# A three-stage TensorE kernel on one core: projections in couples on halves of the rows, and the last tile's first row block in three parts

## What is computed

```python
Kf  = einsum('bjd,ed->bje', F, K_w)
S   = einsum('bid,bjd->bij', F, Kf)
out = einsum('bij,ijd->bid', S, W) + einsum('bid,ed->bie', F, Q_w)
```

## Time and profile before

| | |
|---|---|
| median of 3 runs | 607.16 us (607.0 to 607.43) |
| profiled execution, its own time | 606.42 us |
| its span, first to last instruction | 604.6 us |
| granted TensorE clock, mean | 0.998 of 2.4 GHz |
| busy: TensorE, VectorE, ScalarE | 596.4, 399.2, 401.5 us |
| moved by DMA | 138.12 MB, mean 228 GB/s |

### The profile page before, as it was taken

One profiled execution on the slowest core, in us unless ns is written; L12 is line 12 of the kernel. 1 busy time (PEld: TensorE's weight loads), 2 busy tenths in 40 slices (PEclk: granted clock), 3 DMA queues, 4 the chain that ended last, 5 costly groups with the idle time before them and its releaser, 6 DMA issues.

```text
span 604.6 us, 17904 instructions
## 1 busy us (share of the span) xinstructions
PE 596.4 (99%) x7690; PEld 526.3 (87%) x7690; DVE 399.2 (66%) x412; ACT 401.5 (66%) x696; POOL 0.2 (0%) x4
## 2 busy tenths in 40 slices
PE   9999999999999999999999999999999999999995
PEld 7888989889898898988989898898988989889895
DVE  6556768567685675947749475685756768567486
ACT  7888393874938659295692947939387493865920
POOL 0000000000000000000000000000000000000000
PEclk9999999999999999999999999999999999999999
DMA  8644847457575575755657566484754857557177
GB/s 338 262 141 160 330 165 282 183 185 305 191 281 172 210 266 208 279 196 210 242 192 287 203 238 249 143 319 174 277 209 173 318 179 284 173 209 273 70 281 279
DMA packets 29452, 138.12 MB, mean 228 GB/s; under 512 B 3264, under 2 KB 3776, under 8 KB 21312
## 3 DMA queue, kind: packets, MB, share of 16 engines
q1 hardware_dynamic: 20736, 75.83, 31.8%
q10 hardware_dynamic: 8640, 61.15, 28.4%
HBM read 69.86 MB, written 67.11 MB: 227 GB/s over the span
## 4 chain that ended last, share of the span: by engine, by line
PE 98%; DVE 1%; issue 1%; DVEq 0%
PE ps L509 20%; PE ps L447 20%; PE ps L449 19%; PE ps L448 19%; PE ps L541 18%; DVE o_sb L372 1%; PE ps L576 1%; DVEq L49 0%; DVE o_sb L382 0%; PE ps L467 0%; PE ps L465 0%; PE ps L469 0%; DVE f_hi L388 0%; DVEq L115 0%
## 5 line engine op out<-in xcount | busy, mean ns | idle before, releaser
L337 DVE TENSOR_TENSOR f_lo<-f_ring,f_hi 128x1024 fp32r<-128x1024 f32 x124 | 151.8, 1224 | 168.2 <-ACT f_hi L217 166.6
L231 ACT ACTIVATE q_out<-ps 128x512 f32<-128x512 f32 x256 | 156.9, 613 | 6.6 <-PE ps L449 0.2
L222 ACT ACTIVATE kf<-ps 128x512 f32<-128x512 f32 x256 | 155.8, 609 | 3.5
L372 DVE TENSOR_TENSOR o_sb<-ps,q_out 128x1024 f32<-128x1024 f32 x127 | 145.1, 1215 | 19.4 <-PE ps L541 19.3
L240 ACT ACTIVATE s_t<-ps 128x512 f32<-128x512 f32 x32 | 19.1, 598 | 175.8 <-PE ps L509 175.8
L509 PE MATMUL ps<-f_ring,kf 128*64 128x64 f32 x4096 | 123.5, 222 | 0.3 <-issue 0.3
L509 PEld LDWEIGHTS ps<-f_ring,kf 128*64 128x64 f32 x4096 | 121.1, 138 | 2.6 <-issue 0.8
L541 PEld LDWEIGHTS ps<-s_t,w_sb 64*128 64x128 f32 x2048 | 115.6, 188 | 5.6 <-issue 5.6
L541 PE MATMUL ps<-s_t,w_sb 64*128 64x128 f32 x2048 | 118.6, 274 | 0.0
L447 PE MATMUL ps<-f_hi,k_hi 128*128 128x512 f32 x255 | 101.0, 396 | 0.0
L447 PE MATMUL ps<-f_hi,q_hi 128*128 128x512 f32 x256 | 100.0, 391 | 0.0
(11 more groups left out here) (39 smaller groups left out, 160.3 us busy)
## 6 DMA issues: line engine op xcount, KB each, us to landing
out<-o_sb SPq DMA_DIRECT2D x127, 512.0 KB, 3.5
f_ring<-f_t ACTq DMA_DIRECT2D x58, 1024.0 KB, 4.8
f_ring<-f_t SPq DMA_DIRECT2D x4, 1024.0 KB, 10.6
f_ring<-f SPq DMA_DIRECT2D x8, 256.0 KB, 5.3
w_sb<-w SPq DMA_DIRECT2D x1, 2048.0 KB, 17.8
out<-o_sb SPq DMA_DIRECT2D x2, 256.0 KB, 2.6
o_sb<-first SPq DMA_DIRECT2D x1, 192.0 KB, 2.9
o_sb<-first ACTq DMA_DIRECT2D x1, 192.0 KB, 3.4
```

The source lines that it names most:

```text
L222: nc.scalar.activation(kf[:, c // 2, c % 2 * CK:(c % 2 + 1) * CK, :, :].rearrange("d k h i -> d (k h i)"), ps[:, 2 * c % 8, :], COPY).then ...
L231: nc.scalar.activation(q_out[:, t % 2, :, :].rearrange("d i (h b) -> d i h b", h=2)[:, :, :, at:at + CK], q_bank(t * CHUNKS + c).rearrange ...
L337: nc.vector.tensor_tensor(f_lo[:, v % SPLIT, :], f_unit(v), f_hi[:, v % SPLIT, :].bitcast(F32), ALU.subtract).then_inc(flo_done, 1)
L372: nc.vector.tensor_tensor(o_sb[:, n % OBUF, :, :, :].rearrange("d x s b -> d s x b"), ps[:, bank:bank + 2, :].rearrange("d s (x b) -> d s ...
```

## The change

The projection of the tiles 1 to 15 is issued in couples. A couple is two matmuls of 64 rows each, one on the lower, one on the upper half of TensorE's rows, into two different banks. A chunk's two products (a: Q, b: K) are made in two halves of three couples: first a on the lower rows beside b on the upper rows, then b on the lower beside a on the upper. Between the two halves of chunk n - 1 stand the first halves of chunk n: the order is first(0), first(1), second(0), first(2), second(1), and so on, and at the end first(15), second(14), second(15). Each second half waits on TensorE for half_done. In the last tile, whose last two Q products still run later in the old form, the last step couples K of chunk 14 with K of chunk 15. Tile 0 keeps the old form.

FILL changes to 74, 220 and 284, and its waits lie between the chunks 3 to 15. The splits wait for k_done beside q_done. In the last tile ScalarE copies only the last Q product; the one before is copied by VectorE. The first row block of the last tile goes in three parts, row 0, row 1, and rows 2 and 3, to the banks 0, 2 and 6 (and the next odd ones), with three sums and three stores; the banks and waits of the blocks behind it change with that.

```diff
-FILL = {1: 0, 2: 56}
-FILL.update((t, 108) for t in range(3, TILES - 1))
-FILL[TILES - 1] = 132
+EARLY = 3
+FILL = {1: 74, 2: 220}
+FILL.update((t, 220) for t in range(3, TILES - 1))
+FILL[TILES - 1] = 284
...
-            return [0, 6, 4, 0, 2, 6, 4, 0][k] if t == TILES - 1 else 2 * k % 8
+            return [0, 4, 0, 2, 6, 4, 0, 2][k] if t == TILES - 1 else 2 * k % 8
+        block_0 = [(0, 1, 0), (1, 1, 2), (2, 2, 6)]
...
             def split_f(v):
                 act.wait_ge(q_done, 2 * (v - SPLIT) + 2)
+                act.wait_ge(k_done, 2 * (v - SPLIT) + 2)
...
-                act.wait_ge(k_done, t * CHUNKS + c + 1)
+                act.wait_ge(k_done, n + 1 if n < TILES * CHUNKS - LATE else TILES * CHUNKS)
...
-            for c in range(CHUNKS - LATE, CHUNKS):
-                copy_q(t, c)
+            copy_q(t, CHUNKS - 1)
...
+            c = CHUNKS - 2
+            at = c * CK
+            dve.wait_ge(q_done, TILES * CHUNKS - 1)
+            nc.vector.tensor_copy(
+                q_out[:, t % 2, :, :].rearrange("d i (h b) -> d i h b", h=2)[:, :, :, at:at + CK],
+                q_bank(t * CHUNKS + c).rearrange("d (k h i) -> d i h k", k=CK, h=2)).then_inc(q_copied_dve, 1)
+
             n = t * UNITS
-            dve.wait_ge(o_half, 1)
-            dve.wait_ge(q_copied, TILES * CHUNKS)
+            dve.wait_ge(q_copied, TILES * CHUNKS - 1)
+            dve.wait_ge(q_copied_dve, 1)
             dve.wait_ge(o_stored[n % OBUF], n // OBUF * 16)
-            half_sum(0).then_inc(out_half, 1)
+            for part in range(2):
+                dve.wait_ge(o_part, part + 1)
+                part_sum(part).then_inc(out_part, 1)
             dve.wait_ge(o_done, n + 1)
-            half_sum(1).then_inc(out_done, 1)
+            part_sum(2).then_inc(out_done, 1)
...
+            def products(step):
+                if step < TILES * CHUNKS - LATE:
+                    return (q_of(step), q_done), (k_of(step), k_done)
+                return (k_of(step), k_done), (k_of(step + 1), k_done)
...
+            def passes(dst, w_hi, w_lo, c, rows, first):
+                hi = f_hi[rows, c // 2 % SPLIT, piece_cols(c)]
+                lo = f_lo[rows, c // 2 % SPLIT, piece_cols(c)]
+                yield nc.tensor.matmul(dst, w_hi[rows, :], hi, start=first, stop=False)
+                yield nc.tensor.matmul(dst, w_hi[rows, :], lo, start=False, stop=False)
+                yield nc.tensor.matmul(dst, w_lo[rows, :], hi, start=False, stop=not first)
+
+            def first_halves(step):
+                (a, _), (b, _) = products(step)
+                for ins_a, ins_b in zip(passes(*a, lower, True), passes(*b, upper, True)):
+                    pass
+                ins_a.then_inc(half_done, 1)
+                ins_b.then_inc(half_done, 1)
+
+            def second_halves(step):
+                pe.wait_ge(half_done, 2 * (step - CHUNKS + 1))
+                (a, a_sem), (b, b_sem) = products(step)
+                for ins_b, ins_a in zip(passes(*b, lower, False), passes(*a, upper, False)):
+                    pass
+                ins_b.then_inc(b_sem, 1)
+                ins_a.then_inc(a_sem, 1)
...
+                    if c >= 4 and n < TILES * CHUNKS - LATE:
                         pe.wait_ge(q_copied, n - 3)
-                    if t < TILES - 1 or c < CHUNKS - LATE:
-                        q_product(n)
-                    if t >= 1:
-                        for x in range(FILL[t] * c // CHUNKS, FILL[t] * (c + 1) // CHUNKS):
-                            pe.wait_ge(zeros_done, 1)
+                    first_halves(n)
+
+                    if c >= 1:
+                        second_halves(n - 1)
+
+                    a, b = max(c - EARLY, 0), CHUNKS - EARLY
+                    for x in range(FILL[t] * a // b, FILL[t] * max(c + 1 - EARLY, 0) // b):
+                        pe.wait_ge(zeros_done, 1)
+                if t >= 1:
+                    second_halves(min((t + 1) * CHUNKS - 1, TILES * CHUNKS - LATE))
...
-                    at, col = (bank + 2 * (x // 2), x % 2 * P) if split else (bank, x * P)
+                    at, col = (block_0[min(x, 2)][2], max(x - 2, 0) * P) if split else (bank, x * P)
...
-                    if t == TILES - 1 and k >= 3:
-                        pe.wait_ge(out_half if k == 3 else out_done, 1 if k == 3 else t * UNITS + k - 3)
+                    if t == TILES - 1 and k in (2, 3):
+                        pe.wait_ge(out_part, k - 1)
...
-                    elif k == 2:
-                        pe.wait_ge(q_copied, TILES * CHUNKS)
+                    elif k == 1:
+                        pe.wait_ge(q_copied, TILES * CHUNKS - 1)
+                        pe.wait_ge(q_copied_dve, 1)
```

More of the change, by code:

```diff
@@ L97, in build @@
         fhi_done, flo_done = sem("fhi_done"), sem("flo_done")
+        half_done = sem("half_done")
+        q_copied_dve = sem("q_copied_dve")
         k_done, kf_copied = sem("k_done"), sem("kf_copied")
@@ L191, in _ @@
             slot = t * UNITS % OBUF
[L192 to L196, removed]
+            for part, (x, rows, _) in enumerate(block_0):
+                if part < 2:
+                    sp.wait_ge(out_part, part + 1)
+                else:
+                    sp.wait_ge(out_done, t * UNITS + 1)
+                sp.dma_start(out[t, 0, :, 2 * x * P:2 * (x + rows) * P],
+                             o_sb[:, slot, x:x + rows, :, :].rearrange("d x s b -> d (x s b)")).then_inc(o_stored[slot], 16)
             for k in range(1, UNITS):
@@ L199, in _ @@
             for n in range(OBUF):
-                uses = len(range(n, TILES * UNITS, OBUF)) + (1 if n == slot else 0)
+                uses = len(range(n, TILES * UNITS, OBUF)) + (2 if n == slot else 0)
                 sp.wait_ge(o_stored[n], 16 * uses)
@@ L208, in split_first @@
                 wait(act, q_done, 2 * (c // 2 - SPLIT) + 2)
+                wait(act, k_done, 2 * (c // 2 - SPLIT) + 2)
                 nc.scalar.activation(f_hi[:, c // 2 % SPLIT, piece_cols(c)], f_cols(c), COPY).then_inc(fhi_first, 1)
@@ L225, in copy_q @@
             def copy_q(t, c):
-                act.wait_ge(q_done, t * CHUNKS + c + 1)
+                n = t * CHUNKS + c
+                act.wait_ge(q_done, n + 1 if n < TILES * CHUNKS - LATE else TILES * CHUNKS)
                 if c == 0:
@@ L328, in both_first @@
                 wait(dve, q_done, 2 * (c // 2 - SPLIT) + 2)
+                wait(dve, k_done, 2 * (c // 2 - SPLIT) + 2)
                 if c == 4:
@@ L376, in sum_out, with part_sum @@
                     ALU.add).then_inc(out_done, 1)
-            def half_sum(half):
+            def part_sum(part):
                 t = TILES - 1
-                m = half * (IR // 2)
+                x, rows, bank = block_0[part]
                 return nc.vector.tensor_tensor(
-                    o_sb[:, t * UNITS % OBUF, m:m + IR // 2, :, :].rearrange("d x s b -> d s x b"),
-                    ps[:, 2 * half:2 * half + 2, 0:BANK // 2].rearrange("d s (x b) -> d s x b", x=IR // 2),
-                    q_out[:, t % 2, :, :].rearrange("d (s m) b -> d s m b", s=2)[:, :, m:m + IR // 2, :],
+                    o_sb[:, t * UNITS % OBUF, x:x + rows, :, :].rearrange("d x s b -> d s x b"),
+                    ps[:, bank:bank + 2, 0:rows * P].rearrange("d s (x b) -> d s x b", x=rows),
+                    q_out[:, t % 2, :, :].rearrange("d (s m) b -> d s m b", s=2)[:, :, x:x + rows, :],
                     ALU.add)
@@ L542, in row_block @@
                                                start=True, stop=True)
-                    if split and x == IR // 2 - 1:
-                        ins.then_inc(o_half, 1)
+                    if split and x < 2:
+                        ins.then_inc(o_part, 1)
                 ins.then_inc(o_done, 1)
```

22 lines of the change are left out of this document (17 added, 5 removed).

## The result

The change made the kernel slower, by 0.3%: 609.36 us median (606.97 to 610.68, 6 runs) against 607.58 for the kernel before (607.0 to 608.16, 6 runs), ratio 1.003, 95% interval 1.0018 to 1.0042. The forecast was 594.3 us, its range 590.0 to 606.3. The profiled execution took 606.97 us with a span of 605.2; it is the fastest of the six, so the trace shows 2.4 us less than the median run holds.

The account below looks back on a forecast made before the run. TensorE, busy 99% of the span, was taken to bound the kernel. Savings of 12.0 and 2.8 us less costs of 1.8 and 0.1 made 12.9 us, so 594.3 us from the median 607.16; range 590.0 to 606.3.

Parts of the forecast that it names:

- The couples (the main term): Projection on TensorE: coupled half-row matmuls step in 218.3 ns in place of 226.7, saving 12.0 us.
- no gain in the step: Projection: extra 13.4 ns may be the fp32r weight swap, so couples save nothing; 605.4 us, chance 0.17.
- The slower rival, halves one after the other: Projection: the two halves don't run side by side, a couple takes 431.7 ns; about 900 us, chance 0.03.
- The change of form: Between projection, row blocks and scores: 0.19 us of switching lost today goes, 15 times, saving 2.8 us.
- The late fifth sum: End of the row blocks: scores wait for VectorE's delayed fifth sum, 0.12 us, 14 times; 1.8 us given back.
- Instructions and code: TensorE's sequencer: more instructions and waits, about 78 code fetches; cost set at nothing, bounds -0.5 and +4 us.
- late code: Rival: code fetches stall TensorE 0.27 us at two borders in each tile, 8 us; 602 us, chance 0.05.
- half_done, copies and splits: Projection: the new wait has 0.44 us in reserve, copies and splits behind it 0.4 us; cost nothing.
- the rival of late chains: Projection: ScalarE's and VectorE's copies come late, chunks 6, 10, 14 wait, 6.8 us; 601 us, chance 0.06.
- The end: Last tile: three part sums in place of half sums cost one instruction more, +0.1 us.

Follow-up runs that it names:

- forms: The changed kernel with projections of single tiles in other forms (256 columns, bf16, fp32, one half alone, column halves, whole array); only step times read, 225 to 429.2 ns at 512 columns.
- split_first: The changed kernel with ScalarE's split of the next tile's unit 1 put ahead of chunk 13's copies; 605.90 us, ratio 0.9988 to the kernel before.
- low_twice: The kernel before, with VectorE making the low part of the next tile's unit 1 twice, so sums come later; 608.14 us, ratio 1.0024.
- the second profile: Profile of the changed kernel measured again unaltered, in a later set of runs; median 607.47 us, ratio 1.001, profiled span 606.7 us.
- sf_earlier8: split_first with its code borders 8 instructions earlier, by the count of filling waits; 611.01 us, ratio 1.0057 to the kernel before.

## Why the prediction was wrong

**The couples (the main term): wrong, and it decides.** The step that failed is "I take the extra that both coupled stages show, 5 ns: 218.3 ns". Measured 226.7 ns: the 12.0 us were nothing. Both stages from which I took the 5 ns differ from the projection in two things, couples and fp32 operands at two cycles a column, and I gave the saving to the couples. forms shows that it goes with the latter: 429.2 ns a step in fp32, with couples and without. This was the rival "no gain in the step", for which I took 0.17; "the 13.4 ns may belong to the swap of an fp32r weight" was its reason and is wrong too (bf16 has it), and its 605.4 us missed by 4 us, of which 2.2 are added stalls in the profiled run. The slower rival, halves one after the other, fell: half a couple alone takes as long as the couple.

**The change of form: right.** 2.8 us forecast. Projections and row blocks got 2.29 us shorter together, and split_first, where the sums wait for nothing, shows 2.7 (327.79 + 108.61 against 328.90 + 110.18).

**The late fifth sum: right in kind, too large.** The first sum came at 1.48 us (forecast 1.5), and the scores' loads wait for the sums 13 times:

```profile
PEld ps L584 <- DVE o_sb L388: 2.1, 13, 0.2
```

The loads run ahead of their matmuls, so of these 2.1 us only 0.57 reach the chain (109.18 against 108.61 us of row blocks), not 1.8. What I missed is that a later sum can also move TensorE's code fetch, by 0.24 us in low_twice.

**Instructions and code: the count right, the cost wrong.** 78 fetches as forecast, and the filling waits cost nothing. But "each tile keeps its two borders in the scores at the same place. I set nothing" failed: the fetch of a border depends on more than its place. Stalls rose from 0.95 to 3.2 us in the profiled execution and to 5.1 in the second profile, by 2.2 and 4.1; my upper bound was 4. I had the mechanism as the rival "late code", 0.27 us at two borders in each tile; it stalls at one border, in some tiles, by up to 0.9 us. The Trainium skill calls the crossing of a block "mostly hidden" (Runtime: NRT & Kernel Launch, Instruction fetch mechanics). The traces disagree where the two borders of the scores lie 256 instructions, 3.8 us, apart: over the kernels of the table a fetch takes 0.88 to 1.85 us and starts 1.1 to 3.8 us into the stage.

**half_done, copies and splits: right.** Neither of these waits appears in the projections of the later tiles, so the rival of late chains fell as well.

**The end: too small.** +0.1 us forecast. The parts took 0.06 more, as thought, but the profiled execution ends 0.42 us later, all of it behind the last sum, and in each trace with the new end that piece is longer than in any with the old one. I had looked only at VectorE.

**The account.** The forecast's sum was -12.9 us. By measured terms it is 0 - 2.86 + 0.57 + 2.2 of stalls + 0.6 at start and end = +0.5 us, the difference of the two spans. The median run of the first comparison is 1.8 us slower, and the profiled run was the changed kernel's fastest. More and longer stalls are likely the rest: the second profile has 1.9 us more of them in a run 1.6 us longer. The median run itself has no trace.

**What stays open.** Why the kernels with couples have more late fetches than the one with whole-array matmuls (5 to 8 of 15 against 1). They differ in two things that weren't tried apart, twice the matmuls in TensorE's queue and five code blocks a tile in place of four. Also what makes a single fetch early or late: the place of the border and the time of the sums both matter, and shifts of 8 instructions one way and 5 the other made it worse for no reason that these runs show. The counts of late fetches and the stalls come from one trace each, and two traces of the changed kernel differ by 1.9 us.

## What to carry to other kernels

Take the fixed cost of a TensorE step from matmuls of the same type and the same cycles per column, not from others that happen to run in couples; here couples on halves of the rows only saved the change of form, 0.18 us a time. A new order on a copying engine can move TensorE's code fetches, as low_twice shows: count the idle of TensorE that waits for nothing (issue) in each version, and measure several executions, since it varies from run to run. Where a kernel of this kind gains or loses under 1%, the places of its code borders can be all of it; eight instructions cost 0.7% here, from split_first to sf_earlier8.

## What the hardware showed unexpectedly

- A matmul of one cycle a column takes N/2.4 + 13.3 ns from start to start with its own weight load, at 256 columns in couples and at 512 in couples, on half the rows alone and on the whole array, in fp32r and bf16 (11.7 for bf16 on the whole array). The fp32 ones, at two cycles a column, carry 2.5 ns at 512 columns, in couples and on the whole array, and 5 ns in the couples of scores and row blocks.
- One copy more on VectorE, which brought the first sum 0.27 us later, made TensorE's code fetches start 0.24 us later, with TensorE's code unchanged (low_twice). Bringing the sums 0.38 us forward in the changed kernel didn't bring the fetches forward (1.79 and 1.78 us).
- Behind a stall on code TensorE's next matmul started 1.24 to 1.61 us after the fetch had landed, in all twelve traces.
- Moving the code by 33 instructions made the starts of the fetches 1.0 to 1.2 us later and the kernel 1% slower; moving it 8 the other way put ten of 15 fetches at 2.35 to 2.43 us and made split_first 0.7% slower.
